# One-hots in one evacuation of 128 partitions, put in place by SyncE's DMA; input halves and norm broadcasts issued by GpSimd

## The reference

```python
feat = jnp.concatenate([jnp.broadcast_to(x_i, x_j.shape), x_j - x_i], axis=-1)
h = jnp.einsum('bnkc,oc->bnko', feat, ew) + eb
h = jax.nn.gelu(h * es + et, approximate=False)
h = jnp.max(h, axis=2)
```

## Time and profile before

| | |
|---|---|
| median of the runs | 4033.5 us |
| profiled execution | 4031.99 us, its span 4030.2 us, mean granted clock 0.991 |
| busy PE, DVE, ACT, POOL | 3878.9, 3809.2, 3687.3, 925.9 us |
| DMA | 271.18 MB, 67 GB/s on average |
| queue 0 (issued by GpSimd), queue 1 (by SP) | 26.9% and 7.5% of the 16 engines' time |

### The profile page before, as it was taken

How to read it: one execution, slowest core, us unless ns; L and a number is a source line. 1 busy time by engine, 2 the same in 40 slices (tenths; PEclk the granted TensorE clock), 3 DMA queues, 4 the chain that set the end, 5 groups by cost and what they waited for, 6 DMA issues and landing times.

```text
span 4030.2 us, 67572 instructions
## 1 busy us (share of the span) xinstructions
PE 3878.9 (96%) x22752; PEld 2044.8 (51%) x22752; DVE 3809.2 (95%) x5162; ACT 3687.3 (91%) x6806; POOL 925.9 (23%) x1060
## 2 busy tenths in 40 slices
PE   6999999999999999999999999999999999999984
PEld 3445555555555555555555555555555555555442
DVE  3699999999999999999999999999999999999996
ACT  4899999999999999999999999999999999999983
POOL 1122222222222222222122222222222122222223
PEclk9999999999999999999999999999999999999996
DMA  2133342433333333342333333333342343332333
GB/s 61 23 68 67 70 80 57 79 64 67 74 68 69 62 77 67 64 86 51 78 72 67 72 70 67 64 78 67 60 90 51 68 82 66 68 72 53 60 67 66
DMA packets 99994, 271.18 MB, mean 67 GB/s; under 512 B 14946, under 2 KB 23394, under 8 KB 93476
## 3 DMA queue, kind: packets, MB, share of 16 engines
q0 software_dynamic: 65536, 184.58, 26.9%
q1 hardware_dynamic: 34116, 82.27, 7.5%
HBM read 77.68 MB, written 25.69 MB: 26 GB/s over the span
## 4 chain that ended last, share of the span: by engine, by line
PE 85%; ACT 6%; DVE 5%; issue 3%; DMA 1%; POOL 0%; POOLq 0%; ACTq 0%; SPq 0%; DVEq 0%
PE pg L648 22%; PE pmisc L576 11%; PE pg L651 10%; PE pvu L635 10%; PE pmisc L562 9%; DVE acc L1040 4%; PE pvu L621 3%; PE pmisc L512 3%; PE pmisc L542 3%; PE pmisc L519 3%; PE pmisc L578 3%; PE pmisc L547 2%; PE pmisc L534 2%; ACT MV L810 2%; PE pmisc L536 2%
## 5 line engine op out<-in xcount | busy, mean ns | idle before, releaser
L1040 DVE SCALAR_TENSOR_TENSOR acc<-hpad,w,acc 128x1024 f32<-128x1024 f32 (+1 forms) x2304 | 2621.2, 1162 | 17.4 <-ACT acc L840 14.8
L648 PE MATMUL pg<-MV,VU 128*128 128x512 f32 x2048 | 1138.8, 638 | 29.0 <-issue 25.9
L827 ACT ACTIVATE g<-pg 128x512 f32<-128x512 f32 x1536 | 913.2, 595 | 104.4 <-PE pg L651 75.8
L1018 DVE TENSOR_REDUCE hid<-g 128x192 f32<-128x1536 f32 x512 | 891.7, 1742 | 0.0
L427 POOL DMA_DIRECT2D acc<-tapped x256 | 297.3, 1161 | 2096.3 <-DVE acc L1040 1787.8
L810 ACT ACTIVATE MV<-pvu,cst 64x512 f32<-64x512 f32 x1024 | 696.4, 680 | 9.5 <-PE pvu L621 0.4
L576 PE MATMUL pmisc<-acc,w 128*96 128x256 f32 x2048 | 496.9, 386 | 48.6 <-ACT acc L857 34.0
L651 PE MATMUL pg<-MV,VU 128*64 128x512 f32 x2048 | 527.5, 592 | 0.0
L562 PE MATMUL pmisc<-x,w 96*128 96x512 f32 (+1 forms) x1024 | 510.5, 600 | 8.7 <-ACT hpad L769 8.7
L635 PE MATMUL pvu<-wVU,y 97*64 97x192 f32 x4096 | 446.7, 339 | 22.0 <-ACT MV L810 21.7
L576 PEld LDWEIGHTS pmisc<-acc,w 128*96 128x96 f32 x2048 | 331.0, 165 | 260.0 <-issue 121.3
(11 more groups left out here) (102 smaller groups left out, 4380.5 us busy)
## 6 DMA issues: line engine op xcount, KB each, us to landing
acc<-tapped POOLq DMA_DIRECT2D x256, 512.0 KB, 5.1
xin<-in_x_dram SPq DMA_DIRECT2D x32, 768.0 KB, 6.2
invb<-rows_dram SPq DMA_DIRECT2D x32, 768.0 KB
x<-in_x_dram POOLq DMA_DIRECT2D x128, 192.0 KB, 4.8
res<-x POOLq DMA_DIRECT2D x128, 192.0 KB, 5.3
out_dram<-res SPq DMA_DIRECT2D x128, 192.0 KB, 3.1
hpad<-hpad SPq DMA_DIRECT2D x112, 33.0 KB, 1.8
g<-in_consts_dram SPq DMA_DIRECT2D x1, 640.0 KB
```

The costliest lines, as they stand in the source:

```text
L648: last = nc.tensor.matmul(ps[:, :], VU[:, r, part, 0:ONE128], cols[part], start=True, stop=True)
L827: nc.scalar.activation(g[:, p % 2, part, :, :], pg[(3 * p + part) % 2][:, :].rearrange("p (n k) -> p n k", k=KN), ACT.Gelu).then_inc(gelu_ ...
L1018: nc.vector.tensor_reduce(hid[:, c % 2, j, :, :], g[:, r], op=ALU.max, axis=AX.X).then_inc(hid_ready, 1)
L1040: nc.vector.scalar_tensor_tensor(out=dst, in0=src, scalar=wk, in1=dst, op0=ALU.mult, op1=ALU.add).then_inc(tap_done, 1)
```

## The change

1. A new tile `onehots` (128 x 512). ACT's `onehot` writes it in one instruction of 128 partitions. Before it ACT waits no longer for the gathers of P-2 (`gather_ready`), but until the moves of pair P-1 are done (`onehot_moved`).
2. SP gets `move_onehots`: it waits for those gathers and for `onehot_ready`, and issues two DMAs of 64 partitions of 2 KB each into MV. It does so at every pair, ahead of halo copies and store.
3. PE's gather(P, 0) waits for `onehot_moved` (32 for each pair) in place of `onehot_ready`; `values` waits for `onehot_ready` as before.
4. `load_half` goes to GpSimd: both halves of image 0 as its first instructions, the others at the end of pairs 1 and 8. Of `broadcast_norms` SP keeps the store of the rows (`store_norms`); GpSimd issues the two reads at p mod 16 = 10, ahead of `keep`.
5. The upper halo copy moves from offset 2 to 3, the store from the w2 part's offset + 2 to + 3.
6. `hpad` becomes one row dimension for all groups, with 10 rows in place of 18 for the half group; `rows_of(g, first, end)` gives the slice. This makes room for `onehots`. The instructions on it keep their shapes.

```diff
-UPPER_AT, LOWER_AT = {2: FULL}, {5: FULL}
+UPPER_AT, LOWER_AT = {3: FULL}, {5: FULL}
-STORE_AT = {o + 2: q for o, q in W2_AT.items() if q % 2 == 1}
+STORE_AT = {o + 3: q for o, q in W2_AT.items() if q % 2 == 1}
+def rows_of(g, first, end):
+    return slice((STRIP + 2) * g + first, (STRIP + 2) * g + end)
+        onehots = sb("onehots", [128, KN * NODES])
-        hpad = sb("hpad", [128, 5, STRIP + 2, PADW])
+        hpad = sb("hpad", [128, FULL * (STRIP + 2) + STRIP // 2 + 2, PADW])
...
+            def store_norms(b, p, bi, h):
                 fb, fp = when(b, p, ROWS_AT - 8)
                 sp.wait_ge(misc_evac, job_at(fb, fp, "inv", 4 * h))
                 sp.sem_inc(sp_passed, 1)
                 sp.dma_start(rows_dram.rearrange("k (r n) -> (k r) n", n=128), norm_rows[:, :]).then_inc(rows_stored, 16)
+
+            def move_onehots(P, p):
+                if due(count := 3 * P - 3):
+                    sp.wait_ge(gather_ready, count)
+                sp.sem_inc(sp_passed, 1)
+                if due(count := P + 1):
+                    sp.wait_ge(onehot_ready, count)
+                sp.sem_inc(sp_passed, 1)
+                for w in range(2):
+                    h = 64 * w
+                    sp.dma_start(MV[h:h + 64, p % 2, w, :], onehots[h:h + 64, :]).then_inc(onehot_moved, 16)
...
                     if p % 16 == ROWS_AT and valid(b if h else b + 1, B):
-                        broadcast_norms(b, p, b if h else b + 1, h)
-                    if p in (1, 8) and valid(b, B) and valid(b + 1, B):
-                        ...
-                        load_half(b + 1, h)
+                        store_norms(b, p, b if h else b + 1, h)
+                    if valid(P + 1, NPAIRS):
+                        move_onehots(P + 1, p + 1)
...
         def _(pool):
+            def load_half(b, h):
+                nc.gpsimd.dma_start(xin[:, h, :], xv[b, :, h * 4 * CW:(h + 1) * 4 * CW]).then_inc(xin_load[h], 16)
+            load_half(0, 0)
+            load_half(0, 1)
+            pool.wait_ge(expo_ready, 1)
+            def broadcast_norms(bi, h):
+                n = 2 * bi + h
+                pool.wait_ge(rows_stored, 16 * (n + 1))
+                pool.sem_inc(pool_passed, 1)
+                if due(count := 4 * n):
+                    pool.wait_ge(xn_ready, count)
+                pool.sem_inc(pool_passed, 1)
+                rows = invb[:, :, :].rearrange("p c n -> p (c n)")
+                nc.gpsimd.dma_start(rows[0:C, :], rows_dram[0:1, :].to_broadcast([C, 4 * CW])).then_inc(rows_loaded, 16)
+                nc.gpsimd.dma_start(rows[C:C + 1, :], rows_dram[1:2, :]).then_inc(rows_loaded, 16)
...
+                    if p % 16 == ROWS_AT + 1 and valid(bi, B):
+                        broadcast_norms(bi, h)
...
+                    if p in (1, 8) and valid(b, B) and valid(b + 1, B):
+                        if due(count := CHUNKS * b + 4 * (p // 8) + 4):
+                            pool.wait_ge(ysq_ready, count)
+                        pool.sem_inc(pool_passed, 1)
+                        load_half(b + 1, p // 8)
...
                     if valid(P, NPAIRS):
-                        if due(count := P + 1):
-                            pe.wait_ge(onehot_ready, count)
+                        if due(count := 32 * (P + 1)):
+                            pe.wait_ge(onehot_moved, count)
...
             def onehot(P, p):
                 act.wait_ge(onehot_in, P + 1)
-                if due(count := 3 * P - 3):
-                    act.wait_ge(gather_ready, count)
-                for w in range(2):
-                    h = 64 * w
-                    last = nc.scalar.activation(MV[h:h + 64, p % 2, w, :].rearrange("p (n k) -> p n k", k=KN),
-                                                pone[h:h + 64, :, :].rearrange("p k n -> p n k"), ACT.Relu,
-                                                bias=nbias[h:h + 64, :], scale=1.0)
-                last.then_inc(onehot_ready, 1)
+                if due(count := 32 * P):
+                    act.wait_ge(onehot_moved, count)
+                nc.scalar.activation(onehots[:, :].rearrange("p (n k) -> p n k", k=KN), pone.rearrange("p k n -> p n k"),
+                                     ACT.Relu, bias=nbias, scale=1.0).then_inc(onehot_ready, 1)
```

More of the change, by code:

```diff
@@ L371, in image @@
                         if t == 0:
-                            sp.dma_start(hpad[0:64, gr, 0, 1:W + 1], zrow[0:64, :]).then_inc(kept_half, 16)
+                            sp.dma_start(hpad[0:64, (STRIP + 2) * gr + 0, 1:W + 1], zrow[0:64, :]).then_inc(kept_half, 16)
                         else:
-                            sp.dma_start(hpad[0:64, gr, 0:2, :], hpad[64:128, gr, 8:10, :]).then_inc(kept_half, 16)
+                            sp.dma_start(hpad[0:64, rows_of(gr, 0, 2), :], hpad[64:128, rows_of(gr, 8, 10), :]).then_inc(kept_half, 16)
                     for o, t, s, gr in due_in(LOWER_AT, b, p):
@@ L378, in image @@
                         sp.sem_inc(sp_passed, 1)
-                        sp.dma_start(hpad[64:128, gr, 0:2, :], hpad[0:64, gr, 8:10, :]).then_inc(kept_half, 16)
+                        sp.dma_start(hpad[64:128, rows_of(gr, 0, 2), :], hpad[0:64, rows_of(gr, 8, 10), :]).then_inc(kept_half, 16)
                     for o, t, s, q in due_in(STORE_AT, b, p):
@@ L416, in keep @@
                 if t == 0:
-                    nc.gpsimd.tensor_copy(hpad[:, gr, 0, 1:W + 1], zrow[:, :]).then_inc(kept, 1)
+                    nc.gpsimd.tensor_copy(hpad[:, (STRIP + 2) * gr + 0, 1:W + 1], zrow[:, :]).then_inc(kept, 1)
                 else:
-                    nc.gpsimd.tensor_copy(hpad[:, gr, 0:2, :], hpad[:, gr, STRIP:STRIP + 2, :]).then_inc(kept, 1)
+                    nc.gpsimd.tensor_copy(hpad[:, rows_of(gr, 0, 2), :], hpad[:, rows_of(gr, STRIP, STRIP + 2), :]).then_inc(kept, 1)
             def add_product(t, s, gr):
@@ L757, in shared_evac @@
                         h = 128 if gr < FULL else HALF
-                        nc.scalar.activation(hpad[0:h, gr, 1, 1:W + 1], ps[0:h, 0:W], ACT.Relu, bias=sh[0:h, :],
+                        nc.scalar.activation(hpad[0:h, (STRIP + 2) * gr + 1, 1:W + 1], ps[0:h, 0:W], ACT.Relu, bias=sh[0:h, :],
                                              scale=sc[0:h, :]).then_inc(misc_evac, 1)
@@ L767, in shared_evac @@
                         if m == 1 and t == STRIPS - 1:
-                            nc.scalar.activation(hpad[:, gr, STRIP + 1, 1:W + 1], zrow[:, :], ACT.Copy)
-                        nc.scalar.activation(hpad[:, gr, r0:r1, 1:W + 1],
+                            nc.scalar.activation(hpad[:, (STRIP + 2) * gr + STRIP + 1, 1:W + 1], zrow[:, :], ACT.Copy)
+                        nc.scalar.activation(hpad[:, rows_of(gr, r0, r1), 1:W + 1],
                                              ps[:, 0:(r1 - r0) * W].rearrange("p (row col) -> p row col", col=W),
@@ L773, in shared_evac @@
                         act.wait_ge(kept_half, 32 * s + 16)
-                        nc.scalar.activation(hpad[64:128, gr, 9, 1:W + 1], zrow[64:128, :], ACT.Copy)
+                        nc.scalar.activation(hpad[64:128, (STRIP + 2) * gr + 9, 1:W + 1], zrow[64:128, :], ACT.Copy)
                         for h, n in ((0, 8), (64, 7)):
                             last = nc.scalar.activation(
-                                hpad[h:h + 64, gr, 2:2 + n, 1:W + 1],
+                                hpad[h:h + 64, rows_of(gr, 2, 2 + n), 1:W + 1],
                                 ps[h:h + 64, 0:n * W].rearrange("p (row col) -> p row col", col=W),
@@ L840, in tap0 @@
                 nc.scalar.activation(acc[:, t % 2, sums_of(gr, 0, rows * W)].rearrange("p (row col) -> p row col", col=W),
-                                     hpad[:, gr, 0:rows, 0:W], ACT.Copy, scale=wd[:, gr, 0:1]).then_inc(tap0_done, 1)
+                                     hpad[:, rows_of(gr, 0, rows), 0:W], ACT.Copy, scale=wd[:, gr, 0:1]).then_inc(tap0_done, 1)
             def tap_product(b, p, s, gr):
```

27 lines of the change are left out of this document (6 added, 21 removed).

## The result

| | before | after |
|---|---|---|
| median of the runs | 4033.3 us (4 runs) | 4896.2 us (4 runs, 4888.3 to 4900.8) |
| ratio, 95% interval | 1 | 1.2138 [1.212, 1.2156] |
| profiled execution, span | 4032.0, 4030.2 us | 4888.3, 4886.4 us |
| mean granted clock | 0.991 | 0.896 |

Slower, as forecast, but by 863 us instead of 165, and far outside the range (4065 to 4330). The page of the kernel after: busy times [against rows 1], the granted clock in 40 slices, the chain by engine [against rows 3], three groups and two kinds of DMA issue. L674 is the gather that was L648, L834 the one-hot that was L810 [against rows 4].

The account below looks back on a forecast made before the run. TensorE (PE) was taken to set the pace. Against the profiled 4032.0 us, 133 + 34 + 12 - 17 + 3 = +165 gave 4197, with the median of the runs 4198; own range 4080 to 4290, overall range 4065 to 4330.

Parts of the forecast that it names:

- The bound and the place: PE sets the pace; its stall for the moves comes before the gather in one pair of every eight, pair 2.
- the edits booked at nothing: Other edits, such as GpSimd's broadcast issues and the later halo copy and store: no cost seen, each with its cover.
- near 3340: ACT's busy time after the change, with 348 us of its 3687 gone through single one-hot evacuations.
- where 2.6 was booked: Quiet pairs: both moves land about 2.6 us after the activation ends, hidden within 3.5 us.
- the landing in pair 2: Contention adds 2.4 us (1.1 to 4.2) to the moves, which land at 2047.7 against a gather at 2045.4.
- where 133 stood: Pair 2 of 58 strips: PE waits 2.3 us each, +133 us (58 to 240).
- booked only against pair 3 (43 x 0.8): 768 KB ahead of the last acc<-tapped in three of four strips delays the next pair: +34 us (0 to 86).
- The rival with whole big DMAs: Moves in pair 2 wait for the rest of an acc<-tapped: 4.1 us of stall, 4352 us; chance 0.11.
- The granted clock stays at 1.00 in the middle images: Sign for TensorE after the change: no fall of the clock, since PE stays over 90% busy.
- just enough: Pair 2 when quiet: 2.7 us from the activation's end to the gather, for moves landing after about 2.6.
- "hidden" rival at 4005: Both moves land within 2.7 us in pair 2, so only PE's idle time changes: about 4005 us; chance 0.11.
- booked at 17 us: Single one-hot evacuation on ACT shortens PE's idle time before gathers: -17 us, between 0 and -33.

Follow-up runs that it names:

- no_moves: The changed kernel without the moves: ACT writes the one-hots straight into MV in two instructions, the other edits kept; 4038.6 us, 1.0014 of the kernel before.
- small_beside: The kernel before, plus one 16 KB DMA by SP at the move's moment in pair 2 of each strip, PE waiting for it; 4563.1 us, 1.1313.
- one_move: The changed kernel with only window 1's one-hots moved, by one DMA of 64 rows, window 0's written in place by ACT; 4741.4 us, 1.1757.
- tiny_loads: The changed kernel with GpSimd's 768 KB input halves and broadcasts cut to 8 columns from the second image on; 4706.3 us, 1.1668.
- loads_sp: The changed kernel with input halves and broadcasts back on SP's queue at their old places; 4701.4 us, 1.1656.
- skip2: The changed kernel without moves in pair 2 of each strip, where ACT writes the one-hots straight into MV; 4373.6 us, 1.0855.
- stall2: The kernel before, with PE waiting in pair 5 of 63 strips for two 16 KB DMAs that SP issues one after another; 4479.4 us, 1.1107.
- stall4: The kernel before, with PE waiting in pair 5 of 63 strips for four 16 KB DMAs that SP issues one after another; 4729.2 us, 1.1727.
- tiny_all: The changed kernel with GpSimd's loads, broadcasts and also its accumulating DMAs cut to 8 columns; 4128.5 us, 1.0236.
- hybrid4: The changed kernel with moves only in pair 4 of each strip, input halves and broadcasts on SP's queue; 4025.9 us, 0.9982.

## Why the prediction was wrong in size

**The bound and the place were right.** PE sets the pace, the loss lies in PE's wait for the moves in pair 2 of each strip, and DVE's wait for scores grew with it (140.6 to 965.2 us). ACT's waits for tap_sum did not (29.4 to 29.7 us), and no_moves confirms that the edits booked at nothing cost next to nothing. ACT's busy time is 3386.7 us instead of "near 3340": the one-hots did what was booked (696.4 to 350.7), 45 us came on other activations, off the path. A quiet move lands after 2.18 us, the second, issued 0.5 later, after 2.33: together they are there 2.9 us after the activation's end, where 2.6 was booked.

**The step that failed first: the landing in pair 2.** "To the 128 rows of both moves it adds between 1.1 and 4.2 ... I take 2.4." It adds 3 to the first and 7 to the second. The wait is 7.2 us a strip instead of 2.3: 58 x 7.2 = 418 us where 133 stood (441 over all 64 strips), the larger part of the 541.5. Three readings led there. The range was scaled from the row count of the rows read, and those rows were taken from DMAs issued 0.4 us before to 3.4 us after the gather of pair 2, while the moves are issued 2.6 before it. The lateness doesn't go by the bytes: 16 KB at the moves' own moment are 3.6 us late (small_beside), one move 4.4 (one_move). The 192 KB transfers were counted as the lighter ones, and cutting them helped most. And the 768 KB that the change itself puts ahead of acc<-tapped was booked only against pair 3 (43 x 0.8), where the wait of pair 2 hides it; it makes pair 2 longer (tiny_loads, loads_sp: 195 us with its clock). Where pair 2 doesn't wait, that term shows as 3.1 us in each of the three strips that have it (skip2), four times what was booked.

The rival with whole big DMAs came nearer: it took the 6.0 us of hpad<-zrow, 16 KB, as it stands, and small_beside has 5.3 us for 16 KB. The halo copies said the same with their 5.9 at most. It was set aside for two rows of 4.0 and 4.9 us, and no row told which to take: the trace of before has none at the moves' own moment. Even this rival, with its 4.1 us of wait, gave only 4352.

**The term that was not there: the clock.** "The granted clock stays at 1.00 in the middle images, since PE stays over 90% busy." It is 0.89 over a middle image, and 0.52 to 0.64 in the mean in the pairs behind the four waits. Price: 358 us of busy time in the kernel after. That share of the loss had no term and no rival. A busy share over an image says nothing about this; what counted was the single wait, and the pairs behind it. It answers with 5.0 and 5.6 us a strip in pair 2 (small_beside, the kernel after) and with 2.1 to 2.6 in pair 5 (stall2 to stall4). Why the two places differ stays open: after the wait in pair 2 PE stays at 0.52 through the whole pair, in pair 5 it is back within it (0.72), though it is fully busy in both. The Trainium skill (TensorE: Matmul & The Clock Gate, HAM oscillation — how this bites in real kernels) describes this very thing, matmul groups that each start at the lower level again since PE waited for a DMA between them. The trace of the kernel after agrees for its long waits: behind all 64 of 3 us and more the next pair's clock is under 0.9; of the 35 between 1 and 2 us one is followed by such a pair.

**The quiet margin of pair 2 was not "just enough".** The moves need 2.9 us there, and 2.7 were to be had. tiny_all, where next to nothing of GpSimd's stands in the way, still waits 0.5 to 1.8 us and pays for the clock in some strips: 95 us together. So the "hidden" rival at 4005 would not have come about without GpSimd's bytes either.

**The sum again, with what was measured.** For an image: 28.8 (pairs 2) + 21.4 (clock) + 4.0 (other pairs) = 54.2 of the 54.8 us seen; the first and the last image lose 34.8 and 47.6, the other fourteen 54.9 in the mean, the start 5.3. Together they make up the span's 856. Of the other pairs, 15 waits the 0.7 us that was booked at 0.8; 8 and 31 wait 1.2 and 1.4 us that had no term.

## What to carry to other kernels

Before you put a DMA on the path of the engine that sets the pace, look for the smallest DMAs of the same queue in that stretch of the old trace, and take their longest landing, unscaled by bytes, as the least for yours: here 16 KB after 5 to 6 us foretold the first move (5.25), though not the second (9.4). Where the trace has none at the very moment, put one there: small_beside is such a probe. Then price the wait twice, once for itself and once for TensorE's clock behind it (here 2 to 6 us for each wait of 3 us and more). Moving 0.68 us of work a pair off an engine that is not the bound was booked at 17 us and could give 33 at the most, and gave 7 in hybrid4, which moves only in pair 4.

## What the runs showed of the hardware

- A DMA of 16 KB within SBUF lands after 1.7 us in quiet and 5.3 us (3.0 to 7.2) beside queued accumulating DMAs of GpSimd, with its first packet after 1.1 and 2.9 us; the two of 128 KB after 2.2 and 2.3 us, or 5.25 and 9.4 (up to 13.1).
- At their places in pair 2, two accumulating DMAs of 192 KB held up SP's moves more than those of 512 KB: cutting the former brought the second move's landing from 6.40 to 3.43 us, cutting the latter to 4.85.
- TensorE's granted clock, where it fell, did so within 2 to 5 us of a stop. Behind a wait of 1.8 us the next pair ran at 0.51 in one image and at 1.00 in the next. The return took 3.2 to 6.6 us of full work in pair 5 and 7 to 16 in pair 2.
- The price of the clock did not grow with the wait: 2.5, 2.6 and 2.1 us behind waits of 4.6, 7.3 and 9.05 us.
